# Moving the second attention's key projections out of the head of a fused kernel, and storing them in 2 KB pieces

## The reference

```python
# block 0: 16 heads of 8, batch 8, "positions" 256; softmax over s
q = einsum('oc,bct->bot', Wq, ln(x)) + bq ; k = einsum('oc,bcs->bos', Wk, ctx) + bk ; v = ...
dot = mask * (q.k / sqrt(8)) - (1 - mask) * 1e6
x = x + (softmax(dot) * mask) @ v
...
# block 2 ("the second attention"): 16 heads of 128, 8 batches of 128 tokens
k = (ctx @ Wk).reshape(b, 128, 16, 128)            # depends on inputs alone
x = x + (softmax(q.k / sqrt(128)) @ v) @ Wo
```

## Time and profile before

| | |
|---|---|
| median of 3 runs | 1271.44 us (1271.03 to 1273.45) |
| profiled execution | 1272.62 us, of it 1270.8 us from the first to the last instruction (the span) |
| PE busy | 1086.5 us, 85% of the span |
| DVE, ACT, POOL busy | 56%, 40%, 25% |
| step 0, scores | 40.1 us |
| step 24, first turned scores | 90.1 us |
| last scores, step 127 | 210 us |
| end of the first pass | about 232 us |
| block 2 | about 583 to 870 us |

### The profile page before, as it was taken

The page is one execution under the profiler, slowest core; times in us unless marked ns, Lnnn a source line. Parts: engine busy times, 40 slices in busy tenths (PEclk is TensorE's granted clock), DMA queues, the critical chain, the costliest instruction groups (busy, mean ns, idle before and its releaser), DMA issues.

```text
span 1270.8 us, 20090 instructions
## 1 busy us (share of the span) xinstructions
PE 1086.5 (85%) x6858; PEld 811.3 (64%) x6858; DVE 705.5 (56%) x1700; ACT 505.7 (40%) x1785; POOL 320.0 (25%) x440
## 2 busy tenths in 40 slices
PE   5589998899999867888999999996889999985694
PEld 2365555578999735667877878774555666654463
DVE  5166766522122277887556655555656666664434
ACT  1135555432332235665433333332445555552121
POOL 5053431022232234543000000002122222220552
PEclk9689999889999969989999999998999999997797
DMA  6663431499898416000110101130000000000885
GB/s 210 174 201 93 122 107 44 142 355 317 318 327 331 147 42 240 27 1 29 53 35 34 35 34 35 51 113 4 2 1 9 5 5 1 5 5 12 243 251 189
DMA packets 78083, 138.07 MB, mean 109 GB/s; under 512 B 9738, under 2 KB 54554, under 8 KB 71042
## 3 DMA queue, kind: packets, MB, share of 16 engines
q1 hardware_dynamic: 54097, 114.55, 26.9%
q10 hardware_dynamic: 19468, 10.17, 2.9%
q0 software_dynamic: 4416, 12.06, 2.8%
HBM read 115.67 MB, written 20.88 MB: 107 GB/s over the span
## 4 chain that ended last, share of the span: by engine, by line
PE 57%; DVE 19%; issue 8%; ACT 7%; DMA 6%; POOL 1%; ACTq 1%; another core or an unknown queue 0%; SPq 0%; DVEq 0%; POOLq 0%
PE P L974 6%; PE P L984 6%; PE P L1981 4%; PE P L1941 4%; PE P L259 3%; PE P L1932 3%; ACT big L2357 3%; PE P L2074 2%; PE P L2882 2%; DVE small L576 2%; PE P L426 2%; PE P L2080 2%; PE P L387 2%; DVE big L2589 1%; PE P L2127 1%
## 5 line engine op out<-in xcount | busy, mean ns | idle before, releaser
L576 DVE TENSOR_REDUCE small<-P 128x2 f32<-128x512 f32 x128 | 84.4, 682 | 76.1 <-PE P L387 76.1
L139 POOL TENSOR_TENSOR lrs<-lve,mhalf 128x1 f32<-128x1 f32 x64 | 36.6, 572 | 352.2 <-DVE lve L130 320.1
L2268 ACT ACTIVATE big<-P,small 128x128 f32<-128x128 f32 x128 | 45.3, 365 | 128.4 <-DVE small L2448 128.4
L662 ACT ACTIVATE big<-P 128x512 f32<-128x512 f32 x128 | 72.7, 599 | 58.8 <-PE P L407 52.3
L1024 ACT ACTIVATE big<-P,big 128x128 f32<-128x128 f32 x184 | 52.5, 368 | 109.1 <-PE P L974 96.1
L259 PE MATMUL P<-CT,big 128*128 128x256 f32 (+1 forms) x200 | 74.9, 508 | 21.6 <-ACT XNT L235 20.6
L974 PE MATMUL P<-big 128*128 128x128 f32 x736 | 86.2, 275 | 2.2 <-DMA big<-b_w 1.8
L974 PEld LDWEIGHTS P<-big 128*128 128x128 f32 x736 | 84.1, 192 | 2.9 <-DMA big<-b_w 2.2
L984 PE MATMUL P<-big 128*128 128x256 f32 x368 | 83.1, 379 | 0.0
L1126 DVE COPY big<-P 128x256 f32<-128x256 f32 x23 | 9.8, 425 | 127.1 <-PE P L984 127.1
L2587 DVE TENSOR_TENSOR big<-P,big 128x512 f32<-128x512 f32 x40 | 27.6, 690 | 88.5 <-ACT big L2325 88.4
(11 more groups left out here) (388 smaller groups left out, 2555.2 us busy)
## 6 DMA issues: line engine op xcount, KB each, us to landing
big<-b_w SPq DMA_DIRECT2D x23, 1028.0 KB
big<-b_w SPq DMA_DIRECT2D x23, 1024.0 KB
big<-scr_qk SPq DMA_DIRECT2D x96, 96.0 KB
keys_t<-XNT ACTq DMA_DIRECT2D x32, 256.0 KB, 10.2
big<-keys_t SPq DMA_DIRECT2D x8, 1024.0 KB, 5.0
big<-i_wgu SPq DMA_DIRECT2D x23, 352.0 KB
big<-moe_y SPq DMA_DIRECT2D x16, 256.0 KB, 4.2
big<-i_wd SPq DMA_DIRECT2D x23, 176.0 KB
```

The costliest lines, as they stand in the source:

```text
L576: dve.tensor_reduce(negM[:, h, :], P[:, h % 2, :].rearrange("p (c s) -> p c s", c=2), AX.X, ALU.max, negate=True).then_inc(a_max, 1)
L662: act.activation(ER[:, g % 8], P[:, second_bank(i), :].rearrange("p (c t) -> p c t", c=2), ACT.Exp).then_inc(a_e, 1)
```

## The change

Nothing of the keys is left ahead of step 0. The 26 pairs of the first pass stand in a list of steps: 10 pairs in steps 4 to 23, two in each of rows 2 to 7 (halves at h = 5, 8, 11, 14), four in the drain (a half at each even step from 130 to 144). The six pairs in the routing stay. ACT takes a pair one step after its second half and stores it two steps after that. All inputs of the first pass are loaded by SP ahead of `split_out(0)`; the tokens and weights of the keys (CT, `key_weights`) are issued by SP behind the stacks of batches 0, 1 and 2, the mask rows of batches 0 to 2 by ACT. In HBM the keys lie as (half of the batches, g, j, partition, 4 x 128), so a store writes pieces of 2 KB where it wrote pieces of 512 B, and `key_row` reads 2048 pieces of 512 B where it read pieces of 8 KB. Semaphore offsets follow.

```diff
-        KEYS = nc.dram_tensor("keys_t", (B, 128, 4, 4, T), F32, kind="Internal").ap()
-        KP, K0, K1, K2 = 32, 8, 20, 26
+        KEYS = nc.dram_tensor("keys_t", (2, 4, 4, 128, 4 * T), F32, kind="Internal").ap()
+        KP, K0, K2 = 32, 0, 26
+        key_steps = [*range(4, H + 8), *(H * n + h for n in range(2, B) for h in (5, 8, 11, 14)),
+                     H * B + 2, H * B + 4, H * B + 6, H * B + 8, H * B + 10, H * B + 12, H * B + 14, H * B + 16]
+        key_step = {at: (K0 + i // 2, i % 2) for i, at in enumerate(key_steps)}
+        key_taken = {key_steps[2 * i + 1] + 1: K0 + i for i in range(K2 - K0)}
+        key_sent = {key_steps[2 * i + 1] + 3: K0 + i for i in range(K2 - K0)}
...
-            act.dma_start(KEYS[4 * r:4 * r + 4, :, g, j].rearrange("b p t -> p b t"),
-                          k_out[p % 4].rearrange("p (b t) -> p b t", b=4)).then_inc(k_st[p % 4], 16)
+            act.dma_start(KEYS[r, g, j], k_out[p % 4]).then_inc(k_st[p % 4], 16)
...
             for n in range(3):
                 split_out(n)
                 for half in range(2):
                     s0_stack(sp, n, half)
+                if n < 2:
+                    sp.dma_start(CT[:, :, 512 * n:512 * n + 512], ctx_t[:, :, 512 * n:512 * n + 512]
+                                 ).then_inc((k_w[0], k_ct)[n], 16)
+                    key_weights(sp, n)
+            key_weights(sp, 2)
+            key_weights(sp, 3)
...
-            for p in range(K0):
-                key_part(pe, p, 0, 512)
             for step in range(STEPS):
...
-                if step < LEAD:
-                    key_part(pe, K0 + step // 2, D * (step % 2), D * (step % 2) + D)
-                if late_pair(n, h) is not None:
-                    p, u = late_pair(n, h)
-                    if n + 2 < B and h == 5:
+                if step in key_step:
+                    p, u = key_step[step]
+                    if u == 0 and LEAD <= step < H * (B - 2):
                         pe.wait_ge(a_qb, n + 3)
                     key_part(pe, p, D * u, D * u + D)
...
             act.wait_ge(a_exd, 32)
-            for p in range(2, K0):
-                if p in (2, 4):
-                    s0_extra(act, 0, p // 2 - 1)
-                key_take(act, p)
-                key_store(act, p)
+            for n in range(3):
+                for half in range(2):
+                    s0_extra(act, n, half)
             act.wait_ge(a_one, 3)
             act.dma_start(SCR1, onerow).then_inc(a_exd, 16)
...
-            sp.dma_start(e_kr[b % 2], KEYS[b]).then_inc(k_rd[b % 2], 16)
+            cols = slice(T * (b % 4), T * (b % 4) + T)
+            sp.dma_start(e_kr[b % 2], KEYS[b // 4, :, :, :, cols].rearrange("g j p t -> p g j t")).then_inc(k_rd[b % 2], 16)
```

More of the change, by code:

```diff
@@ L214, in build, with keys_before @@
         k_out = [XNT[:, s // 2, 512 * (s % 2):512 * (s % 2) + 512] for s in range(4)]
-        KEYS = nc.dram_tensor("keys_t", (B, 128, 4, 4, T), F32, kind="Internal").ap()
-        KP, K0, K1, K2 = 32, 8, 20, 26
+        KEYS = nc.dram_tensor("keys_t", (2, 4, 4, 128, 4 * T), F32, kind="Internal").ap()
[5 more added lines that the diff above has]
+        key_sent = {key_steps[2 * i + 1] + 3: K0 + i for i in range(K2 - K0)}
+        K1 = K0 + sum(at < H + 8 for at in key_steps) // 2
+        def keys_before(step):
+            return K0 + sum(at < step for at in key_steps) // 2
         def key_place(p):
@@ L262, in key_part @@
                 t.then_inc(k_pe, 1)
[L264 to L268, removed]
         def s0_loads(sp):
@@ L279, in s0_loads @@
                 sp.dma_start(dst, src).then_inc(a_ld, 16)
[L280 to L284, removed]
             sp.dma_start(idf[:, :], ident).then_inc(ld_id, 16)
-            sp.dma_start(CX[:, 2:4, :], ctx_cbt[:, 2:4, :]).then_inc(ld_c, 16)
-            for dst, src in ((wvT, a_wvT), (bvb, rows(a_bv)), (tmT, maskT)):
+            sp.dma_start(X[:, 2:8, :], x_cbt[:, 2:8, :]).then_inc(ld_x, 16)
+            sp.dma_start(CX[:, 2:8, :], ctx_cbt[:, 2:8, :]).then_inc(ld_c, 16)
+            for dst, src in ((wvT, a_wvT), (bvb, rows(a_bv)), (tmT, maskT), (selm, a_sel),
+                             (TMf[:, 2 * D:], rows(mask_row[:, 2 * D:]))):
                 sp.dma_start(dst, src).then_inc(a_ldv, 16)
[L290 to L305, removed]
         def s0_extra(eng, n, half):
@@ L330, in s0_sp @@
         def s0_sp(sp):
+            ctx_t = ctxT.rearrange("(k p) n -> p k n", p=128)
             def split_out(n):
@@ L372, in values @@
                 if n == 0:
-                    pe.wait_ge(a_ldv, 48)
+                    pe.wait_ge(a_ldv, 80)
                 else:
@@ L663, in s0_act @@
                                    ACT.Exp).then_inc(a_e, 1)
-                if step < LEAD and step % 2:
-                    key_take(act, K0 + step // 2)
-                    key_store(act, K0 + step // 2)
+                if step in key_taken:
+                    key_take(act, key_taken[step])
+                if step in key_sent:
+                    key_store(act, key_sent[step])
                 if h == 3 and n + 2 < B:
@@ L672, in s0_act @@
                     values(n)
[L673 to L676, removed]
                 if g == 2 and 0 < m < B:
@@ L694, in split @@
                 if n == 2:
-                    pool.wait_ge(a_ldm, 16)
+                    pool.wait_ge(a_ldv, 80)
                 pool.tensor_tensor(qkf, qkb, TM[:, n:n + 1, :].broadcast_to([128, 2, D]), ALU.mult).then_inc(a_qkf, 1)
@@ L719, in values @@
                     pool.wait_ge(a_zero, 2)
-                    pool.wait_ge(a_ldv, 48)
+                    pool.wait_ge(a_ldv, 80)
                 pool.tensor_tensor(Vt, Vt, bvb.rearrange("p (a d) -> p a d", a=1).broadcast_to([128, 2, 128]),
@@ L1851, in build @@
         k_rd, KRD0 = [ld_c, ld_id], 16
-        h_ld3, HLD30 = a_ldv, 48
+        h_ld3, HLD30 = a_ldv, 80
         def again(eng, sems):
@@ L2028, in third @@
                     if b == 0:
-                        pe.wait_ge(f_ld, FLD0 + 48)
+                        pe.wait_ge(f_ld, 48)
                     for k in range(KD):
@@ L2465, in masks @@
             def masks():
-                dve.wait_ge(m_ld, MLD0 + 16)
+                dve.wait_ge(m_ld, 16)
                 dve.tensor_copy(m_mul, m_u8).then_inc(m_pre, 1)
@@ L2471, in masks @@
                 dve.wait_ge(m_pre, 2)
-                dve.wait_ge(f_ld, FLD0 + 48)
+                dve.wait_ge(f_ld, 48)
             def tables():
-                dve.wait_ge(h_lt, HLT0 + 112)
+                dve.wait_ge(h_lt, 112)
                 dve.tensor_copy(h_cm, h_ca.rearrange("p (a t) -> p a t", a=1).broadcast_to([128, 4, T])).then_inc(h_tab, 1)
@@ L2948, in s8_dve @@
             choose(dve, 1)
-            step, weights_of = route_dve(dve, i_pos, IPOS0, i_rank, IRANK0, m_ld, MLD0 + 48)
+            step, weights_of = route_dve(dve, i_pos, IPOS0, i_rank, IRANK0, m_ld, 48)
             slots_dve(dve, step, i_rank, IRANK0)
```

18 lines of the change are left out of this document (1 added, 17 removed).

## The result

| | changed kernel | kernel before, same chips |
|---|---|---|
| median | 1267.53 us (1263.70 to 1272.41, 19 runs) | 1272.54 us (1268.33 to 1276.57, 19 runs) |
| ratio, 95% interval | 0.9963 [0.9949, 0.9976] | |
| profiled execution, span | 1268.1 us | 1270.8 us |
| step 24, first turned scores | 75.1 us | 90.1 us |
| last scores, step 127 | 201.5 us | 210.0 us |

The ratio is a gain of 0.37%, 4.7 us. The last three lines tell the story of the trace: 15.0 us are won up to step 24, 6.5 of them are given back in the rows (15.0 won at step 24, 8.5 at step 127) and 5.7 in the drain (8.5 at step 127, 2.8 at the last turned scores). 2.8 us are left at the end of the pass, and 2.7 at the end of the span.

A forecast was written before the change was run, and what follows sets the result against it. PE was taken as the engine to watch, idle in the head and nearly full in the rows. Head -17.3, rows +3.7, drain +4.1 sum to -9.5 us: 1262 us forecast, range 1252 to 1271.

The forecast's parts named there:

- The head: Lead up to step 24: first turned scores at 72.8 us instead of 90.1, a gain of 17.3 us (bounds 12 and 25).
- the landing of `split_out(1)`: Head, SP's queue: issued at 30.7 us, landing taken as 5.8 us, between 4.8 (batch 0) and 9.15 (batch 1).
- Both named waits: Head: PE's longest waits at step 4 (some 4 us) and step 12 (until 52 us), for DMAs of weights or CT.
- The rows: Rows 2 to 7, one more pair each: a cost of 3.7 us, 2.7 from a slip of 0.45 a row, 1 for the maxima.
- The maxima, charged at 1 us: Rows: `max_rows` queued behind the new store on ACTq, charged at 0.15 us a row, 1 us in all.
- the 20.5 us named as a sign of being wrong: Rows: the prediction counts as wrong if the rows take 20.5 us or more; 19.5 was expected in rows 2 to 4.
- The drain: Drain, four pairs with 6.9 us of PE work, partly filling idle time: a cost of 4.1 us (bounds 3.3 and 6.9).
- The pieces: Key layout in HBM: block 2's reads in 512 B pieces stay hidden, costed at nothing; by the 512 B rule stores gain nothing.
- That the maxima wait behind the stores: Rival, rows and drain: maxima landing in 6.4 us instead of 2.3, 24.5 us in all, 1286 us; chance 0.07.
- That the moved pairs cost their full price: Rival, rows and drain: 10.4 + 6.9 = 17.3 us, taking all the gain, 1271 us; chance 0.08.
- SP's queue: Rival, head: SP's queue later than forecast, step 12 at 60 us, head gain 9.3 us, 1270 us; chance 0.08.
- Block 2 never waited: Rival, block 2: it waits for its keys, six batches 35 us late each at worst, 1472 us; chance 0.02.

The follow-up runs named there:

- e3: Changed kernel with loads of CT and key weights issued just behind the writes of `split_out(1)` and `split_out(2)`, not ahead: 1263.77 us, ratio 0.9948 to the kernel before.
- e4: Changed kernel with the loads of CT and key weights issued one batch earlier, behind `split_out(0)` and `split_out(1)`: 1262.46 us, ratio 0.9928 to the kernel before.
- e1: Changed kernel with the second pair of each of rows 2 to 7 shrunk to two 8-column matmuls: 1265.07 us, ratio 0.9942 to the kernel before.
- e7: Changed kernel with the store of the second pair of rows 2 to 6 issued behind the maxima's DMAs: 1265.20 us, ratio 0.9953 to the kernel before.
- e5: Changed kernel with the keys' old HBM layout (stores in 512 B pieces, reads in 8 KB): 1266.78 us, ratio 0.9964 to the kernel before.
- e10: e4 with the ones written first on ACT's queue and SP issuing the mask rows of batches 1 and 2: 1242.60 us, ratio 0.9834 to the kernel before.
- e2: Changed kernel with the four pairs of the drain shrunk to 8-column matmuls, copies and stores kept: 1260.00 us, ratio 0.9929 to the kernel before.
- e6: Kernel before with the new key layout alone (stores in 2 KB pieces), no pair moved: 1255.83 us, ratio 0.9892 to the kernel before.
- e9: e6 with the write of the ones issued ahead of key pairs 2 to 7 on ACT's queue: 1245.77 us, ratio 0.9854 to the kernel before.
- e11: e10 with rows' last key-pair stores behind the maxima and SP's expert-input writes behind the last maxima: 1241.56 us, ratio 0.9826 to the kernel before.

## What the prediction had right and what failed

The direction held, and the range (1252 to 1271); the size did not: 9.5 us were forecast, and measured are 2.7 in the span (1268.1 us where 1261.3 was forecast) and 4.7 by the ratio. The miss is in all three terms of the sum, each of them too hopeful: 2.3 us in the head, 2.8 in the rows, 1.6 in the drain.

- **The head, 15.0 us where 17.3 were forecast** (12.5 to 15.0 over the six traces). The step that failed here is the landing of `split_out(1)`: taken as 5.8 us, measured 10.7. Of its two bounds, 4.8 and 9.15 us, I chose near the lower, on the argument that the queue would be less full. e3 shows that it isn't the loads right ahead of it: with them behind, it took 9.3. What e3, e4 and the kernel before have in common is the twelve stack reads of 96 KB right ahead of it; a split with a pause behind them landed in 3.1 us in e3 and 3.3 in e4. So 9.15 us there was the row to take. CT's second half was issued at 49.59 us where 45 was forecast. The landing of the first weight took 10.2 us (30.09 to 40.33) instead of 7.3. Both named waits, at step 4 and step 12, came, with 5.6 and 3.5 us; step 0 came at 30.15 us, not near 28. From the half pair of step 12 to step 24 it took 18.7 us instead of 20.8, which gave 2.1 back: the wait for the maxima was 2.59 us and not 4.98.
- **The rows, 6.5 us where 3.7 were forecast.** The slip of PE was sized rightly: 0.43 and 0.53 us a row where 0.45 was taken, and the pair at 11 and 14 hidden (e1). What the sum lacked are three things. The maxima, charged at 1 us, cost 1.6 us in the five intervals of the changed kernel against e7, and from 0.3 (e5) to 2.1 us (e10) in others; the cause is not settled. One interval, 20.49 us, came within 0.01 us of the 20.5 named as a sign of being wrong. The half at h = 14 of row 7, where no row's scores follow, is not hidden: 0.9 us, of which e1 returns 0.7. And from step 24 to the first `place` there is 1.2 us more (22.3 instead of 21.1), for four more matmuls; that is one of the six slips and some 0.7 us beyond it.
- **The drain, 5.7 us where 4.1 were forecast.** Of the four pairs' 6.9 us of PE work 2.8 were counted as filling idle time; e2 gives 4.9 back, so it was 2.0. The other 0.8 us stay in e2 too, where PE has no wait for the maxima at step 136 and waits 0.69 and 0.16 us for ScalarE's copies. Why the maxima of step 136, issued last at 206.46, were read only at 210.66 in the changed kernel stays open.
- **The pieces, nothing in the changed kernel (e5) and 13.7 us in the kernel before (e6).** For this change the item costed at nothing was right, and so was the reason for the gain in the head: with pieces of 512 B, moving the pairs alone brings step 24 to 75.6 us (e5). What I did not see is that the same wait has a second, cheaper remedy, which leaves the pairs where they are (e6, step 24 at 77.6). The row to see it by was in the same window as the earlier trace rows: issues of 3 to 6 us on ACTq, among rows of 0.4. In the list of waits such time has no releaser but `issue` (7.4 us in one piece for ACT), and I passed over it. I read only the 14.5 us for the ones, which is in part its consequence: in e6 the ones are issued 4.9 us earlier and land 7.3 us later instead of 13.0. The Trainium skill (DMA: Bandwidth & Descriptors, Specifications) puts line rate at 512 B and more; by that rule e6 would equal the kernel before. The measured ratio is 0.9892, and the measurement decides.
- **The rivals.** That the maxima wait behind the stores was small if it was there at all: the changed kernel spends 1.6 us more than e7 and not 24.5, and the landing was 2.6 us at the median and not 6.4. That the moved pairs cost their full price came nearer than the forecast in the drain only. SP's queue was late by half of what its rival had: step 12 got its tokens at 56.4 us, forecast were 52 and the rival's 60. Block 2 never waited.

## What to carry to other kernels

A change of two parts needs both parts run alone: here the part costed at nothing was the better one, and the part that looked like the gain lost 9.0 us once the other was there. In a head that waits, look first for issues that take microseconds and for the small transfer that stands last in the queue of big ones; putting 24 KB ahead of them was worth 3.0 us in e9's trace (4.8 by ratios that overlap), and 11.9 us in e10 together with handing eight mask-row DMAs to the other queue. A window in which the bound engine idles is a place for its work only as long as the wait is there; once the wait can be removed, weigh it anew. e10, with its head emptied of pairs, reaches step 24 13.6 us before e9, and has 2.6 us of that left at the end of the pass. Compare whole times only within one chip.

## What the runs showed of the hardware

**A short wait is paid a second time in the clock.** The stretches behind step 24 (length, busy us and instructions of PE, PEld, DVE, ACT, POOL, granted clock, DMA share, GB/s) in the changed kernel, where PE had waited 2.59 us and then 0.96:

```profile
75.10:97.40 22.30, 20.92 (x163) 12.91 (x163) 13.31 (x24) 13.43 (x26) 10.09 (x15) 0.85 0.31 100
...
78.00:81.00 3.00, 3.00 (x17) 1.78 (x19) 2.50 (x4) 2.07 (x4) 1.16 (x3) 0.50 0.55 186
...
84.00:88.00 4.00, 4.00 (x39) 2.59 (x40) 3.19 (x9) 2.30 (x5) 0.00 (x0) 1.00 0.28 82
```

The same stretch in e10, after waits of 0.42 and 0.96 us:

```profile
61.20:81.00 19.80, 18.23 (x163) 11.46 (x163) 14.29 (x27) 13.25 (x26) 10.60 (x14) 1.00 0.65 188
```

The same 163 matmuls took 20.92 us of PE in one and 18.23 in the other: for some 6 us around and after the longer wait the clock stood at its lower level, 1.2 instead of 2.4 GHz. In e11, with waits of 1.09 and 0.96 us, the stretch had a mean clock of 0.92 and PE was busy for 19.99 us. The kernel before pays this too, after its wait of 4.98 us:

```profile
90.10:111.20 21.10, 20.58 (x159) 12.48 (x159) 12.70 (x24) 12.34 (x23) 7.91 (x12) 0.82 0.25 74
```

So the lost time is a price of the wait ahead of `turned` in both kernels and hardly a part of their difference; a version without the wait gets it back. The price doesn't follow the length of the wait alone: after 2.92 us in e5 the mean clock was 0.80, after 4.12 us in e1 it was 0.85, and in e3, with no wait but 0.96 us for a copy, 0.92.

**An engine can be held in its own issues.** With 256 KB stores of 512 pieces of 512 B, ACT was held for up to 3.0 us in one issue, and two mask-row DMAs among these stores took 6.12 us; with 128 pieces of 2 KB the longest issue of a store past the first was 0.71 us in e6. It isn't short pieces alone: in e9, with pieces of 2 KB, one store's issue took 2.32 us. The reads of 1 MB on SP's queue, in 512 B pieces in the changed kernel, landed in 5.5 us at the median against 5.0 before: there short pieces cost almost nothing. That the fill of the queue decides between the two is an inference from these cases; no run isolates it.
